# Issuing the first gate and up matmuls between the last projections of a fused attention and FFN layer (8 cores)

## The reference, cut to what matters

```python
def reference(x, q_w, kv_w, proj_w, proj_b, w_gate, w_up, w_down):   # x: 1 x 16384 x 1024
    # _L0_attn_ref: q = x @ q_w.T, k and v from x @ kv_w.T,
    #               softmax(q k.T / 8) v inside windows of 256 tokens,
    #               out @ proj_w.T + proj_b
    x = _layernorm(x + _L0_attn_ref(x, q_w, kv_w, proj_w, proj_b), axis=-1)
    # _L0_ffn_ref:  silu(x @ (w_gate/127).T) * (x @ (w_up/127).T), then @ (w_down/127).T
    #               w_gate, w_up: 3072 x 1024, w_down: 1024 x 3072
    x = _layernorm(x + _L0_ffn_ref(x, w_gate, w_up, w_down), axis=-1)
    return x
```

## Time and profile before

| what | us |
|---|---|
| median of 2 runs | 980.89 (980.47 to 981.31) |
| the profiled execution, its own time | 980.74 |
| its span, first to last instruction, slowest core (core 4) | 978.1 |
| spans of the 8 cores | 968.9 to 978.1 |
| PE busy / DVE busy / ACT busy in the span | 798.3 / 320.6 / 235.4 |
| mean granted TensorE clock of the 8 cores, as a share of full speed | 0.892 to 0.901 |

### The profile page before, as it was taken

One profiled execution on the slowest core, in us unless ns is written; L12 is line 12 of the kernel. 1 busy time (PEld: TensorE's weight loads), 2 busy tenths in 40 slices (PEclk: granted clock), 3 DMA queues, 4 the chain that ended last, 5 costly groups with the idle time before them and its releaser, 6 DMA issues.

```text
span 978.1 us, 12054 instructions; the slowest of 8 cores (968.9 to 978.1 us)
## 1 busy us (share of the span) xinstructions
PE 798.3 (82%) x4054; PEld 350.4 (36%) x4128; DVE 320.6 (33%) x538; ACT 235.4 (24%) x741; POOL 74.0 (8%) x150
## 2 busy tenths in 40 slices
PE   3667777654999999957888899776499999999996
PEld 2123333222444444412333344332244444443332
DVE  0147876322121111113555455543312221111111
ACT  0045553121211111103333343422121111111111
POOL 4000000000111111200000010000011111100000
PEclk7568987876999999967999899689699999999998
DMA  8961120322222222271111130122222222211221
GB/s 106 250 165 15 20 55 2 96 65 75 65 76 76 76 76 79 46 117 44 44 44 44 44 87 33 44 68 93 87 65 69 83 76 77 75 33 38 75 72 64
DMA packets 33354, 68.93 MB, mean 70 GB/s; under 512 B 4240, under 2 KB 4240, under 8 KB 33296
## 3 DMA queue, kind: packets, MB, share of 16 engines
q0 software_dynamic: 23920, 42.74, 18.9%
q1 hardware_dynamic: 9376, 25.43, 8.0%
HBM read 50.86 MB, written 12.58 MB: 65 GB/s over the span
## 4 chain that ended last, share of the span: by engine, by line
PE 64%; DMA 12%; DVE 8%; issue 7%; ACT 6%; POOL 1%; SPq 0%; DVEq 0%; ACTq 0%; POOLq 0%
PE ps L265 61%; DMA wqsb<-wq 6%; DMA x<-xtm 5%; PE ps L382 3%; ACT pool L350 2%; DVE silu L707 2%; DVE pool L397 2%; DMA xbf<-xfm 2%; ACT r L715 2%; DVE r L707 2%; ACT silu L715 1%; DVE x2s L725 1%; DVE pool L421 0%; ACT lnst L719 0%; DVE xbf L470 0%
## 5 line engine op out<-in xcount | busy, mean ns | idle before, releaser
L265 PE MATMUL ps<-wdres,hbuf 128*128 128x512 bf16 x745 | 183.4, 388 | 10.3 <-issue 1.5
L265 PE MATMUL ps<-xbf,wgw 128*128 128x512 bf16 x752 | 182.7, 383 | 4.0 <-DVE xbf L470 2.9
L265 PE MATMUL ps<-xbf,wuw 128*128 128x512 bf16 x752 | 180.4, 380 | 0.8
L589 DVE SCALAR_TENSOR_TENSOR hbuf<-ps,silu 128x512 bf16<-128x512 f32 x96 | 66.4, 692 | 271.8 <-PE ps L265 266.0
L350 ACT ACTIVATE pool<-ps 128x256 bf16<-128x256 f32 x256 | 97.9, 383 | 116.2 <-PE ps L265 91.8
L584 ACT ACTIVATE silu<-ps 128x512 f32<-128x512 f32 x96 | 57.3, 597 | 267.2 <-PE ps L265 267.1
L265 PEld LDWEIGHTS ps<-wdres,hbuf 128*128 128x128 bf16 x768 | 70.6, 99 | 113.3 <-issue 43.8
L265 PEld LDWEIGHTS ps<-xbf,wgw 128*128 128x128 bf16 x768 | 75.5, 99 | 95.5 <-issue 7.2
L265 PEld LDWEIGHTS ps<-xbf,wuw 128*128 128x128 bf16 x768 | 75.3, 98 | 91.4 <-issue 1.4
L367 DVE SCALAR_TENSOR_TENSOR pool<-pool,rr 128x1024 bf16<-128x1024 bf16 x64 | 78.4, 1225 | 6.7
L265 PE MATMUL ps<-xbf,wqsb 128*128 128x512 bf16 x246 | 72.7, 434 | 7.5 <-DMA wqsb<-wq 2.2
(11 more groups left out here) (55 smaller groups left out, 350.2 us busy)
## 6 DMA issues: line engine op xcount, KB each, us to landing
wgw<-wg POOLq DMA_DIRECT2D x48, 256.0 KB, 2.6
wuw<-wu POOLq DMA_DIRECT2D x48, 256.0 KB, 2.6
x<-xtm SPq DMA_DIRECT2D x16, 512.0 KB, 3.8
y<-x SPq DMA_DIRECT2D x16, 512.0 KB, 2.9
wdres<-wd POOLq DMA_DIRECT2D x1, 6144.0 KB, 49.7
wqsb<-wq POOLq DMA_DIRECT2D x18, 256.0 KB, 4.6
xbf<-xfm POOLq DMA_DIRECT2D x16, 256.0 KB, 13.1
x2scr<-x2s SPq DMA_DIRECT2D x16, 256.0 KB, 2.1
```

What stands on the lines that cost most here:

```text
L265: last = t.matmul(o, l, r, start=st_, stop=sp, tile_position=tpos)
L589: return v.scalar_tensor_tensor(H_sb[:, m, n * 512:(n + 1) * 512], bank(6)[:, 0:512], FS, silu_sb[:, par, n * 512:(n + 1) * 512], ALU.mult ...
```

## The change

In `emit_projseg` the 24 matmuls of three groups (gate and up of slice 0, half 0; gate of slice 1, half 0) are issued between the projections. `gu_unit` is split in its matmuls (`gu_mm`) and its ACT and DVE part (`gu_ev`). Gate and up of slice 0 go behind the transposes of token tile 3 and ahead of the projection of tile 6; gate of slice 1 goes behind the transposes of tile 4 and ahead of the projection of tile 7. Silu and H of slice 0 are issued behind the copy of tile 7, and ahead of up of slice 1. The units of half 1 for slices 0 and 1 follow; before, slice 0 had both halves, then slice 1. Loads of the weights of slices 2 and 3 stay with the units (0, 1) and (1, 1). From slice 2 on nothing differs.

```diff
-            for wt in range(4, NBLK * 2):
-                emit_proj_ln(st, wt)
-                emit_x2t(st, wt - 2)
-            emit_x2t(st, NBLK * 2 - 2)
-            emit_x2t(st, NBLK * 2 - 1)
-            for m in range(HC):
+            emit_proj_ln(st, 4)
+            emit_x2t(st, 2)
+            emit_proj_ln(st, 5)
+            emit_x2t(st, 3)
+            gu_mm(st, 0, 0)
+            emit_proj_ln(st, 6)
+            emit_x2t(st, 4)
+            gu_mm(st, 1, 0, which="g")
+            emit_proj_ln(st, 7)
+            emit_x2t(st, 5)
+            emit_x2t(st, 6)
+            emit_x2t(st, 7)
+            gu_ev(st, 0, 0)
+            gu_mm(st, 1, 0, which="u")
+            gu_ev(st, 1, 0)
+            gu_unit(st, 0, 1, pf=True)
+            gu_unit(st, 1, 1, pf=True)
+            for m in range(2, HC):
                 gu_unit(st, m, 0, pf=False)
                 gu_unit(st, m, 1, pf=True)
...
-        def gu_unit(st, m, n, pf=True):
+        def gu_mm(st, m, n, which="gu"):
             par = m % 2
             gb = 5 if par == 0 else 7
...
+            if "g" in which:
...
+                mm_group(g_pairs, f"G m{m} n{n}", reads=XC + (f"wg{par}",),
+                         writes=(f"pb{gb}",))
+            if "u" in which:
...
+                mm_group(u_pairs, f"U m{m} n{n}", reads=XC + (f"wu{par}",),
+                         writes=("pb6",))
+
+        def gu_ev(st, m, n):
+            par = m % 2
+            gb = 5 if par == 0 else 7
             def silu_fn(s_, par=par, n=n, gb=gb):
...
+
+        def gu_unit(st, m, n, pf=True):
+            gu_mm(st, m, n)
+            if pf and m + 2 < HC:
+                emit_ffn_w(st, m + 2, "wg", wgw_sb, wg_d)
+                emit_ffn_w(st, m + 2, "wu", wuw_sb, wu_d)
+            gu_ev(st, m, n)
```

More of the change, by code:

```diff
@@ L563, in emit_ffn_w @@
                   writes=(f"{which}{m % 2}",), note=f"ld {which} m{m} st{st}")
-        def gu_unit(st, m, n, pf=True):
+        def gu_mm(st, m, n, which="gu"):
             par = m % 2
             gb = 5 if par == 0 else 7
[L568 to L582, removed]
+            if "g" in which:
+                g_pairs = [(bank(gb)[:, 0:512], wgw_sb[:, par, k, :],
+                            xbf_sb[:, k, n * 512:(n + 1) * 512],
+                            k == 0, k == DC - 1, None) for k in range(DC)]
+                mm_group(g_pairs, f"G m{m} n{n}", reads=XC + (f"wg{par}",),
+                         writes=(f"pb{gb}",))
+            if "u" in which:
+                u_pairs = [(bank(6)[:, 0:512], wuw_sb[:, par, k, :],
+                            xbf_sb[:, k, n * 512:(n + 1) * 512],
+                            k == 0, k == DC - 1, None) for k in range(DC)]
+                mm_group(u_pairs, f"U m{m} n{n}", reads=XC + (f"wu{par}",),
[3 more added lines that the diff above has]
+            gb = 5 if par == 0 else 7
             def silu_fn(s_, par=par, n=n, gb=gb):
```

## The result

| | before | changed |
|---|---|---|
| median of the runs, us | 981.08 (10 runs) | 994.57 (11 runs) |
| profiled execution: its time / span of the slowest core | 980.74 / 978.1 | 992.15 / 990.6 |
| spans of the 8 cores | 968.9 to 978.1 | 984.4 to 990.6 |

Three of the 11 runs of the changed kernel (1056 to 1108 us) fell in a slower state, in which the cores of one die had a lower granted clock, and every ratio in this document leaves such runs out, which is why this one is smaller than that of the two medians. The ratio is 1.0121 with a 95% interval of 1.0101 to 1.0140. The change costs 11.9 us of 981.1 (9.9 to 13.7). Forecast were 993.5 and +12.6.

The account below looks back on a forecast made before the run. PE bounds gate and up; in the projection stage residual loads behind spills set the pace, leaving PE idle. Super-tiles cost +6.6 and +6.0, so 980.74 + 12.6 = 993.4, or 993.5 us against the median; range 986 to 1001.

Parts of the forecast that it names:

- The place where the first burst starts: Gate and up of slice 0 start 0.2 us after tile 3's copy, at 220.5 and 685.9, none in the gap before.
- The projection queued behind the burst: Tile 6's projection waits behind two groups, 34 matmuls together; its stt starts 6.2 us later, 6.4 in super-tile 1.
- the fill works: Rival: the three groups run wholly in idle PE time in the projection stage, delaying no stt; 971.6 us; chance 0.05.
- The bursts and the stt's: Bursts of 9.67 and 7.94 us in the projection stage make stt 7 late by 11.0 us, 10.9 in super-tile 1.
- the working without slow matmuls: Both bursts wholly at the upper clock level: 7.34 and 5.61 us, super-tiles +2.0 and +1.4, total 984.
- slow matmuls: Matmuls at the lower clock level, 0.427 us against 0.216; 11 taken in each burst after idle PE.
- Behind stt 7: Up of slice 1 waits 0.72 us for H of slice 0; three fewer groups ahead of slice 2 save 5.18.
- silu's wait: A wait of 0.39 us for silu in super-tile 1 goes away.
- The weight loads: Slice 2's gate load has three groups, 5.2 us, and needs 3.1; costed at nothing, worst case 0.7 us.
- The sum by super-tile: Super-tile 0: 11.0 + 0.72 - 5.18 = +6.6; super-tile 1: 10.9 + 0.72 - 5.18 - 0.39 = +6.0.
- the clock that stays low: Rival: lower level through most of both bursts; 999.4 with 18 slow per burst, 1009.5 with all; chance 0.12.
- the clock that stays up: Rival: the clock comes up sooner or stays up in the bursts; 979.5 to 986 us; chance 0.08.

Follow-up runs that it names:

- the kernel with copies ahead: Changed kernel with transposes and copy of tile wt - 2 emitted between projection and layer norm of tile wt (tiles 2 to 7); 974.61 us, ratio 0.9905.
- 36 and 20 added matmuls: Changed kernel with useless matmuls in PE's idle time, 36 ahead of the first inserted burst and 20 ahead of the second; 989.72 us, ratio 1.0082.
- The kernels with PE kept busy: Changed kernel with useless matmuls ahead of both inserted bursts, 26 and 20 or 36 and 20; 992.70 us and 989.72 us.
- 26 added matmuls: Changed kernel with useless matmuls in PE's idle time, 26 ahead of the first inserted burst and 20 ahead of the second; 992.70 us, ratio 1.0086.
- the last kernels: Kernel before plus early residual loads and the three groups behind tile 7's projection: 923.62 us; same with tile 7's copy ahead of up of slice 1: 925.52 us.

## Why the prediction was right, point by point

**The place where the first burst starts.** Held. It stood behind the copy of tile 3, 0.26 us after its end (taken: 0.2), with the gap ahead of it empty. That its place on DVE is what matters is shown by the kernel with copies ahead: same order on PE, and stt 5 to 6 back at 8.6.

**The projection queued behind the burst.** Held, and together with the late copy it is the cause; taking away either one removes the loss. The kernel with the groups behind the projections differs in nothing else, and turns +11.9 us into -10.2. The rival "the fill works" gave 971.6 for the case in which no stt is held up; that kernel, in which none is, ran in 973.4.
The Trainium skill's advice that I had weighed (Perfetto Trace Analysis, Optimization Strategy: weave regimes into each other) was thus neither right nor wrong here. It names no place; the same weaving lost 11.9 us in one place and won 10.2 in another.

**The bursts and the stt's.** From stt 5 to 6 the working gave 8.79 + 6.2 = 15.0 in super-tile 0 and 8.64 + 6.4 = 15.0 in super-tile 1; measured were 15.16 and 14.82. From stt 6 to 7 it gave 13.3; measured were 12.80 and 14.38. Two errors cancel in this. Where all of a burst ran at the upper level, as with 36 and 20 added matmuls, the intervals were 13.04 / 13.04 and 11.30 / 11.66; the working without slow matmuls comes to 12.7 and 11.0. So without the clock it was too short by 1.7 us in the four intervals together. Divided by 0.211, the distance of the changed kernel from there gives 10 and 7 slow matmuls in super-tile 0, and 8 and 13 in super-tile 1, in place of 11 each: 1.2 us too many. The mean was near, the single counts were not. On core 0, super-tile 0, the first burst had 7 (3.38 us for the gate group, 1.89 for up), the second 13 (3.57 for the gate group, and 4.72 where 16 matmuls at the upper level take 3.62: 8 and 5). The kernels with PE kept busy show that this term is clock.

**Behind stt 7.** A term slightly mis-sized. The working gave 25.48 + 0.72 - 5.18 = 21.0 and, with silu's wait, 25.23 + 0.72 - 5.18 - 0.39 = 20.4; measured were 20.0 and 20.7. The wait of PE for H was there (1.65 us in all, 0.6 of it H's own). Its removal brought about 0.3 us, so as a cost of the change the 0.72 was too high. The weight loads showed no wait of PE in the changed kernel: the gate load was issued at 256.56 on core 0, and the groups behind followed each other every 1.73 us, gate of slice 2 (261.04) too.

**The sum by super-tile.** The working gave +6.6 and +6.0. By the medians of the intervals from stt 5 to the fourth H it was (15.16 + 12.80 + 20.04) - (9.27 + 8.60 + 25.48) = +4.7 and (14.82 + 14.38 + 20.66) - (8.64 + 8.66 + 25.28) = +7.3. The total came out right in part because these two differences cancel, and that is luck. In super-tile 0 the base that I worked from, core 4, had a residual load for tile 6 of 3.86 us; four of the other cores had stt 5 to 6 at 9.75 to 10.6, and the insertion hides such long loads. In super-tile 1 the second burst was slow for longer, 14.3 to 14.4 on all cores. From stt 2 to 5, which the change doesn't touch, the medians fell by 1.0 and 0.4 us, so that the whole from stt 2 on grew by 10.0 (149.9 against 139.9 in the median), and the time by 11.9.

**Rivals.** Neither the clock that stays low nor the clock that stays up happened in the changed kernel. The second was made by hand, with 36 and 20 added matmuls, and gave 1.0082: still slower than before. So this change loses even at the upper level. For bursts without slow matmuls the working gave 984, +3.4; the run had +8.0, and from stt 2 to the fourth H the two super-tiles took 5.0 us more than before (144.9 against 139.9). Of the difference to the working, 1.7 us are those named above; the other 3 stay open.

## What to carry to other kernels

Before work is put into an engine's idle time, look for two things: when its last operand is written, in the order in which the writing engine really gets there, and which instruction stands behind it in the queue. A group whose operand comes late is free only behind the instruction that is due next; with the same 24 matmuls and the same copies that is the difference between +12 and -10 us. Ahead of it a group is free only if its operand is there early enough, as with the copies ahead (-9.3 us). And ask first what makes the gap: the load of each tile moved past a spill in SP's queue was worth 46 us, and left only one gap worth filling.

## What the runs showed of the hardware

The length of PE's last idle time did not by itself decide at which level the next matmuls ran. With 26 added matmuls, an idle time of 2.98 us ahead of the burst (core 3) was followed by 8 matmuls in 3.31 us, and one of 2.54 us (core 5) by 8 in 1.89. But on core 2, in super-tile 1, 2.48 us of idle time were followed by 3.48 us, at a granted clock of 0.51:

```profile
684.93 3.48 PE L265 MATMUL ps<-xbf,wgw 128*128 128x512 bf16 x8 [2.48 <-DVE xbf L470]
```

In the last kernels the clock fell without any idle time over 1.2 us. PE did two rounds of 8 transposes (0.61 us each) with gaps of 0.94 us, then had a gap of 1.15 us, and the 8 matmuls behind took 3.25 us. With 0.2 us or less in place of this last gap five of eight cores still had the upper level in super-tile 0, and all eight in super-tile 1. A wait that looks like pure loss can be tied to the clock in this way: of 0.6 us of waiting removed in front of matmuls, 0.4 came back as matmuls at the lower level, and for 0.9 us removed it was 1.4.

With the residual loads in the loop, stt 2 to 5 in the kernel before varied from 25.65 to 30.98 us between cores; with the loads out of it, it was 14.77 or 14.78 on all eight. The metric is the slowest core, so a loop bound by a transfer pays for the worst of eight.
